# Four row buffers and deeper lookahead in the projection of the second graph's rows

## What is computed

```
x2   = x1 + factor * y[kept position of the row]
xn   = (x2 - mean(x2)) / sqrt(var(x2) + 1e-5)
hh   = xn @ W                       # 8 heads of 32
s_src, s_dst = sum over a head of hh * a_src, hh * a_dst
```

## Time and profile before

| | us |
|---|---|
| runs | 5120.07, 5128.81, 5130.25; median 5128.81 |
| profiled execution | 5127.6 |
| its span, first to last instruction | 5125.8 |
| mean granted TensorE clock | 0.861 of full speed |
| busy: PE, DVE, POOL, ACT | 3909.5, 3118.7, 2344.6, 1867.0 |
| stage `project_heads`, from its first instruction (2562.4) to the next stage's (2733.3) | 170.9 |

### The profile page before, as it was taken

How to read it: one execution, slowest core, us unless ns; L and a number is a source line. 1 busy time by engine, 2 the same in 40 slices (tenths; PEclk the granted TensorE clock), 3 DMA queues, 4 the chain that set the end, 5 groups by cost and what they waited for, 6 DMA issues and landing times. The chain is left out here.

```text
span 5125.8 us, 69922 instructions
## 1 busy us (share of the span) xinstructions
PE 3909.5 (76%) x16154; PEld 2806.8 (55%) x16282; DVE 3118.7 (61%) x7733; ACT 1867.0 (36%) x5097; POOL 2344.6 (46%) x2387
## 2 busy tenths in 40 slices
PE   6977777777777659967965777777774349999998
PEld 3555555555555448856843444444443336777776
DVE  3389989999999766662045777777777761111111
ACT  1334444444444213311213555555553303333332
POOL 2265555556555340001045777777773402333332
PEclk8989999999999789987966778787776569999999
DMA  2565555555555232211064444444443441211111
GB/s 75 182 186 160 164 159 160 161 160 165 162 156 160 66 105 92 92 58 41 31 201 129 110 109 110 108 111 110 111 110 86 132 148 29 33 31 31 31 32 27
DMA packets 316121, 553.59 MB, mean 108 GB/s; under 512 B 63430, under 2 KB 213782, under 8 KB 315856
## 3 DMA queue, kind: packets, MB, share of 16 engines
q0 software_dynamic: 137120, 388.63, 28.9%
q1 hardware_dynamic: 178736, 161.98, 10.4%
HBM read 459.75 MB, written 90.62 MB: 107 GB/s over the span
## 5 line engine op out<-in xcount | busy, mean ns | idle before, releaser
L411 POOL DMA_INDIRECT attend_ring<-kv_rows,all_step_src x880 | 867.5, 986 | 592.5 <-PE attend_ps_agg L450 440.0
L914 POOL DMA_INDIRECT edge_ring<-head_rows,all_step_src x880 | 863.9, 982 | 285.2 <-issue 185.5
L950 PE MATMUL edge_ps_agg<-edge_msg,edge_sel 128*128 128x264 f32 x1760 | 644.7, 492 | 208.3 <-DVE graph_acc L1249 105.7
L450 PE MATMUL attend_ps_agg<-attend_msg,attend_sel 128*128 128x264 f32 x1760 | 591.3, 441 | 243.5 <-DVE graph_qa L766 138.1
L2799 DVE TENSOR_TENSOR moe_gl<-moe_ps_h,moe_act 128x341 f32<-128x341 f32 x210 | 107.9, 514 | 776.7 <-PE moe_ps_h L2717 776.7
L950 PEld LDWEIGHTS edge_ps_agg<-edge_msg,edge_sel 128*128 128x128 f32 x1760 | 374.9, 237 | 352.6 <-issue 171.3
L450 PEld LDWEIGHTS attend_ps_agg<-attend_msg,attend_sel 128*128 128x128 f32 x1760 | 317.7, 204 | 415.3 <-DVE graph_qa L766 182.7
L436 PE MATMUL attend_ps_q<-graph_qa,attend_sel_t 128*128 x1760 | 512.2, 419 | 7.1 <-DVE attend_prod L661 6.4
L2717 PE MATMUL moe_ps_h<-experts_w,moe_xt 128*128 x1680 | 501.8, 451 | 0.6 <-ACT moe_xt L2748 0.6
L766 DVE SCALAR_TENSOR_TENSOR graph_qa<-graph_qa,all_step_same,attend_ps_agg 128x264 f32 x880 | 421.8, 479 | 58.8 <-PE attend_ps_agg L450 42.4
L571 ACT ACTIVATE attend_sel<-all_lane,all_step_dst 128x128 f32<-128x128 f32 x880 | 281.2, 390 | 429.6 <-PE attend_ps_agg L450 414.0
(11 more groups left out here) (423 smaller groups left out, 6374.8 us busy)
## 6 DMA issues: line engine op xcount, KB each, us to landing
attend_ring<-kv_rows,all_step_src POOLq DMA_INDIRECT x880
edge_ring<-head_rows,all_step_src POOLq DMA_INDIRECT x880
kv_rows<-qkv_kv SPq DMA_DIRECT2D x25, 512.0 KB, 2.9
experts_w<-in_w_t SPq DMA_DIRECT2D x16, 682.0 KB
attend_mask<-run_starts SPq DMA_DIRECT2D x440, 8.1 KB
edge_mask<-run_starts SPq DMA_DIRECT2D x440, 8.1 KB
head_rows<-hds_hh SPq DMA_DIRECT2D x25, 264.0 KB, 3.4
qkv_x<-in_x SPq DMA_DIRECT2D x25, 256.0 KB, 3.3
```

The costliest lines, as they stand in the source:

```text
L411: nc.gpsimd.indirect_dma_start(ring[:, step % RING1, :], None, g.kv_rows, bass.IndirectOffsetOnAxis(g.step_src[:, step:step + 1], 0)).then ...
L450: nc.tensor.matmul(ps_agg[i % SUM_BANKS][:, 0:AGG], sel[:, q % 2, u % QU, :], msg[:, q % 2, u % QU, :], start=True, stop=True).then_inc(s_ ...
L914: nc.gpsimd.indirect_dma_start(ring[:, n % slots, u, :], None, g.head_rows, bass.IndirectOffsetOnAxis(g.step_src[:, step:step + 1], 0)).th ...
L950: nc.tensor.matmul(ps_agg[i % BANKS][:, 0:AGG], sel[:, q % 2, u % QU, :], msg[:, q % 2, u % QU, :], start=True, stop=True).then_inc(s_agg, 1)
```

## The change

Only `project_heads` changes. Its tiles `r`, `x2`, `xn` and `stat` get four slots instead of two (pair number modulo 4), the turned rows in SBUF and PSUM three; heads and output PSUM keep two. The row numbers of all 25 pairs are converted by one instruction before the first gather. SP loads pairs 0 to 3 at the start (2 and 3 behind the weights) and pair n+4 when pair n is normalized; it stores the heads of pair n-2 in turn n. POOL gathers pairs 0 to 2 at the start and pair n+3 behind the root of pair n; the gather waits for the sum of the pair that had the slot, no longer for its normalization. DVE folds the vectors first, then begins pair n+1 before it ends pair n; sums and statistics count on a semaphore of their own. PE transposes two pairs ahead of the projection, and ScalarE copies turned rows two ahead. All loops are written out, without the hardware loop. Transfers, sizes, matmuls and arithmetic stay as they are.

```diff
@@ -2045,96 +2045,105 @@
 def project_heads(nc, g, s_dst):
+    ROWS, TURNED = 4, 3
     with Phase(nc, "hds") as m:
         w = m.sb("w", [P, KC, AGG + H])
         vec = m.sb("vec", [P, 2, D])
-        r = m.sb("r", [P, 2, 2, 2, D])
...
+        r = m.sb("r", [P, ROWS, 2, 2, D])
+        x2 = m.sb("x2", [P, ROWS, 2, D])
+        xn = m.sb("xn", [P, ROWS, 2, D])
+        xt = m.sb("xt", [P, TURNED, KC, 2, P])
         hh = m.sb("hh", [P, 2, 2, AGG])
         att = m.sb("att", [P, 2, KC, D])
...
+        stat = m.sb("stat", [P, ROWS, 20])
+        idx = m.sb("idx", [P, BLOCKS], I32)
+        ps_t = [m.ps(f"ps_t{i}", [P, 2, KC, P]) for i in range(TURNED)]
         ps_o = [m.ps(f"ps_o{i}", [P, 2, 512]) for i in range(2)]
...
+        s_w, s_ln, s_sum, s_var, s_rstd, s_t, s_xt, s_mm, s_hh, s_fold, s_idx = (
+            m.sem(k) for k in ("w", "ln", "sum", "var", "rstd", "t", "xt", "mm", "hh", "fold", "idx"))
+        s_y = m.sems_of_pool("y", ROWS)
+        s_x, s_st = ([m.sem(f"{k}{i}") for i in range(ROWS)] for k in ("x", "st"))
+        s_hst = [m.sem(f"hst{i}") for i in range(2)]
         block = m.block()
-        LN = 1 + LN_STEPS
+        BEGIN = LN_STEPS
         @block.sync
         def _(sp):
...
+            def load(n):
+                sp.dma_start(r[:, n % ROWS, 0], pair_rows(g.resid, n)).then_inc(s_x[n % ROWS], 16)
+            def store_heads(n):
+                sp.wait_ge(s_hh, n * 2 + 1)
+                sp.dma_start(pair_rows(g.head_rows, n), hh[:, n % 2]).then_inc(s_hst[n % 2], 16)
+            load(0)
+            load(1)
             sp.dma_start(w[:, :, 0:D], g.W.rearrange("(k p) n -> p k n", p=P)).then_inc(s_w, 16)
             for i, a in enumerate((g.a_src, g.a_dst)):
                 sp.dma_start(vec[:, i, :], spread(a.rearrange("h d -> (h d)"), D)).then_inc(s_w, 16)
...
-                    store_heads(n - 1, 1 - slot)
...
+            load(2)
+            load(3)
+            for n in range(PAIRS):
+                sp.wait_ge(s_ln, n + 1)
+                if n + ROWS < PAIRS:
+                    load(n + ROWS)
+                sp.dma_start(pair_rows(g.norm, n), xn[:, n % ROWS]).then_inc(s_st[n % ROWS], 16)
+                sp.dma_start(pair_rows(g.x2, n), x2[:, n % ROWS]).then_inc(s_st[n % ROWS], 16)
+                if n >= 2:
+                    store_heads(n - 2)
+            store_heads(PAIRS - 2)
+            store_heads(PAIRS - 1)
+            for i in range(ROWS):
+                sp.wait_ge(s_st[i], 32 * -(-(PAIRS - i) // ROWS))
+            for i in range(2):
+                sp.wait_ge(s_hst[i], 16 * -(-(PAIRS - i) // 2))
         @block.gpsimd
         def _(pool):
...
-                pool.wait_ge(s_idx, n + 1)
-                pool.nop(nofuse=True)
+            def gather(n):
+                if n >= ROWS:
+                    pool.wait_ge(s_sum, (n - ROWS) * BEGIN + 1)
                 for b in range(2):
...
+                    nc.gpsimd.indirect_dma_start(r[:, n % ROWS, 1, b, :], None, g.kept_y,
+                                                 bass.IndirectOffsetOnAxis(idx[:, n * 2 + b:n * 2 + b + 1], 0)).then_inc(s_y[n % ROWS], 16)
+            def root(n):
                 pool.wait_ge(s_var, n + 1)
...
+                nc.gpsimd.tensor_tensor(stat[:, n % ROWS, 18:20], stat[:, n % ROWS, 16:18], g.minus_half[:], ALU.pow).then_inc(s_rstd, 1)
+            pool.wait_ge(s_idx, 1)
+            gather(0)
+            gather(1)
+            gather(2)
+            for n in range(PAIRS):
+                root(n)
+                if n + 3 < PAIRS:
+                    gather(n + 3)
         @block.vector
         def _(v):
...
-                    v.wait_ge(s_t, n - 1)
+            def begin(n):
+                c, at = Count(v, s_sum, n, BEGIN), n % ROWS
+                v.wait_ge(s_x[at], (n // ROWS + 1) * 16)
+                v.wait_ge(s_y[at], (n // ROWS + 1) * 32)
+                if n >= ROWS:
+                    v.wait_ge(s_st[at], n // ROWS * 32)
                 for b in range(2):
...
+                    ins = nc.vector.scalar_tensor_tensor(x2[:, at, b, :], r[:, at, 1, b, :], g.factor[:, n * 2 + b:n * 2 + b + 1],
+                                                         r[:, at, 0, b, :], ALU.mult, ALU.add)
                 c.then(ins)
...
+                norm_begin(nc, c, stat[:, at], x2[:, at], s_var)
                 c.done()
+            def end(n):
+                if n >= ROWS:
+                    v.wait_ge(s_t, n - ROWS + 1)
+                v.wait_ge(s_rstd, n + 1)
+                for b in range(2):
+                    ins = nc.vector.tensor_scalar(xn[:, n % ROWS, b, :], x2[:, n % ROWS, b, :], stat[:, n % ROWS, 12 + 2 * b:13 + 2 * b],
+                                                  stat[:, n % ROWS, 18 + b:19 + b], ALU.subtract, ALU.mult)
+                ins.then_inc(s_ln, 1)
             def fold():
@@ -2146,70 +2155,66 @@
                     nc.vector.tensor_reduce(w[:, :, D + i * H:D + (i + 1) * H], att[:, i].rearrange("p k (h d) -> p k h d", h=H),
                                             AX.X, ALU.add).then_inc(s_fold, 1)
-            end(begin(0, 0), 0)
             v.wait_ge(s_w, 48)
             fold()
...
-                    end(begin(n + 1, 1 - slot), 1 - slot)
...
+            begin(0)
+            for n in range(PAIRS):
+                if n + 1 < PAIRS:
+                    begin(n + 1)
+                end(n)
         @block.tensor
         def _(pe):
...
+            def transposes(n):
+                pe.wait_ge(s_ln, n + 1)
+                if n >= TURNED:
+                    pe.wait_ge(s_xt, n - TURNED + 1)
                 for b in range(2):
                     for k in range(KC):
...
+                        last = nc.tensor.transpose(ps_t[n % TURNED][:, b, k, :], xn[:, n % ROWS, b, k * P:(k + 1) * P], g.ident[:])
                 last.then_inc(s_t, 1)
...
+            def project(n):
                 pe.wait_ge(s_xt, n + 1)
...
+                if n >= 2:
                     pe.wait_ge(s_hh, n * 2 - 2)
                 for b in range(2):
                     for k in range(KC):
...
+                        last = nc.tensor.matmul(ps_o[n % 2][:, b, 0:AGG + H], xt[:, n % TURNED, k, b, :], w[:, k, :],
                                                 start=(k == 0), stop=(k == KC - 1))
                 last.then_inc(s_mm, 1)
...
+            pe.wait_ge(s_w, 48)
+            pe.wait_ge(s_fold, 4)
+            transposes(0)
+            transposes(1)
+            for n in range(PAIRS):
+                project(n)
+                if n + 2 < PAIRS:
+                    transposes(n + 2)
         @block.scalar
         def _(act):
...
+            def evac_xt(n):
                 act.wait_ge(s_t, n + 1)
...
-                    act.wait_ge(s_y[slot], (n - slot) * 16)
...
-                    index(n + 2, slot)
+                if n >= TURNED:
+                    act.wait_ge(s_mm, n - TURNED + 1)
+                nc.scalar.activation(xt[:, n % TURNED].rearrange("p k b n -> p b k n"), ps_t[n % TURNED][:], ACT.Copy).then_inc(s_xt, 1)
+            def heads(n):
                 act.wait_ge(s_mm, n + 1)
...
+                if n >= 2:
+                    act.wait_ge(s_hst[n % 2], n // 2 * 16)
+                nc.scalar.activation(hh[:, n % 2], ps_o[n % 2][:, :, 0:AGG], ACT.Copy).then_inc(s_hh, 1)
+                nc.scalar.activation(s_dst[:, n * 2:n * 2 + 2, :], ps_o[n % 2][:, :, AGG:AGG + H], ACT.Copy).then_inc(s_hh, 1)
+            nc.scalar.activation(idx[:], g.from_kept[:], ACT.Copy).then_inc(s_idx, 1)
+            evac_xt(0)
+            evac_xt(1)
+            for n in range(PAIRS):
+                heads(n)
+                if n + 2 < PAIRS:
+                    evac_xt(n + 2)
 def graph2_out(nc, g, acc, logits, out):
```

More of the change, by code:

```diff
@@ L2127, in begin @@
                 for b in range(2):
-                    ins = nc.vector.scalar_tensor_tensor(x2[:, slot, b, :], r[:, slot, 1, b, :],
-                                                         g.factor[:, bass.ds(n * 2 + b, 1)], r[:, slot, 0, b, :],
-                                                         ALU.mult, ALU.add)
+                    ins = nc.vector.scalar_tensor_tensor(x2[:, at, b, :], r[:, at, 1, b, :], g.factor[:, n * 2 + b:n * 2 + b + 1],
+                                                         r[:, at, 0, b, :], ALU.mult, ALU.add)
@@ L2131, in begin @@
                 c.then(ins)
-                norm_begin(nc, c, stat[:, slot], x2[:, slot], s_var)
-                return c
-            def end(c, slot):
-                norm_end(nc, c, stat[:, slot], xn[:, slot], x2[:, slot], s_rstd, 0, 1)
+                norm_begin(nc, c, stat[:, at], x2[:, at], s_var)
                 c.done()
+            def end(n):
[6 more added lines that the diff above has]
+                ins.then_inc(s_ln, 1)
@@ L2177, in turn @@
                     for k in range(KC):
-                        last = nc.tensor.matmul(ps_o[slot][:, b, 0:AGG + H], xt[:, slot, k, b, :], w[:, k, :],
```

(22 more changed lines are left out.)

50 lines of the change are left out of this document (removed).

## The result

Runs of the two kernels in turn gave a median of 5090.8 us for the changed one (5086.7 to 5093.8) and 5126.9 us for the one before (5120.1 to 5130.3). The ratio is 0.9930, with a 95% interval of 0.9915 to 0.9945: 36 us faster. Forecast were 5084 and a range of 5063 to 5105. The profiled execution took 5093.7 us, its span is 5091.8, at a mean granted clock of 0.867.

The account below looks back on a forecast made before the run. A loop of waits bound the stage at 6.30 us a pair; the DMA engines would be next, at p = 4.3 us a pair. Stage gain 44.6, so 5127.6 - 44.6 + 1.2 = 5084 us, range 5063 to 5105.

Parts of the forecast that it names:

- The bound before: Stage before the change: no engine or transfer full, a loop of waits through indices, gathers and landing, 6.30 us a pair.
- Pair time: Changed stage: DMA engines bound, SP's bytes 2.88 plus gathers' packet time 1.36 give 4.24, taken as 4.3 us a pair.
- The loop of three pairs: Changed stage, gathers three ahead: POOL's issue 3.1, landing 3.8 and DVE 2.3 need only 3.1 us a pair, no longer the bound.
- the next bound: POOL in the changed stage: root, gap and two gathers take 3.4 us a pair, 4.1 with DVE working beside it.
- POOL or DVE bounds, p = 3.5: Rival for the changed stage: POOL or DVE sets 3.5 us a pair, gain 65, total 5064; chance 0.22.
- Start: Start of the changed stage: vectors land about 3.5 us behind their issue, first pair normalized at 2576.3.
- ScalarE, SP: Changed stage: heads' store lands 5.1 to 6.6 us after normalization, before the buffer's reuse at 7.1; covered, little to spare.
- The stages behind: Stages after the changed one: same code, so costed at nothing.
- signs of being wrong: Whole kernel: DMA share below 0.85 with p above 5, PE unpausing at 0.50, DVE waiting for stores, later stages changing time.
- depth not reached: Rival for the changed stage: some buffer or SP's order holds about 6 us a pair, gain 5, total 5124; chance 0.05.
- PE stays low: Rival for the changed stage: PE stays at its lower clock, 5.1 us a pair, gain 22, total 5107; chance 0.14.
- transfers pile up: Rival for the changed stage: late stores delay sums, needing 11.7 us landing; at 13 us, 27 us slower, 5156; chance 0.04.

Follow-up runs that it names:

- number 7: Kernel before, loops written out, indices of all pairs converted by one copy and the gathers' wait for them gone; ratio 0.9962, stage 154.9 us.
- 2: Kernel before, with the stage's hardware loops written out as Python loops on all five engines; ratio 1.0009, stage 169.0 us.
- number 5: Kernel before, semaphores declared so that all later ones get the changed kernel's numbers, all work as before; ratio 1.0016, stage 167.2 us.
- number 8: Changed kernel with gathers two pairs ahead instead of three, everything else kept; ratio 0.9957, stage 139.9 us.
- number 3: Changed kernel without the store of x2, the output stage reading the normalized rows instead; ratio 0.992, stage 105.6 us at 3.46 a pair.
- number 6: Changed kernel with 23 idle instructions on POOL behind its last root; ratio 0.9902, stage 110.0 us, edge stage 1417.7 us.
- number 11: Changed kernel again, unaltered, for a second trace; 5441.0 us against 5499.9 for the kernel before, ratio 0.9902.
- number 9: Changed kernel with two pairs gathered at the start instead of three, the third behind the first root; 5499.5 us beside 5493.6 for the kernel before.
- 12: Changed kernel with gathers three pairs ahead up to pair 20 and two ahead for the last four; ratio 0.9896, stage 115.7 us.
- 10: Changed kernel with two more gathers, whose data nobody reads, behind the last root; 5434.0 us beside 5493.6 for the kernel before, stage 112.4 us.

## Why the prediction was right, and where it was not

**The bound before: right.** The stage was a loop of waits. Opening its first edge alone gives 12 to 14 us (number 7 against 2 and 5); taking the normalization out of it as well, with the change's buffers and orders, brings the stage to 139.9 (number 8); the third pair of depth to 110.

**Pair time: the mis-sized term.** The step that failed is "SP's bytes at 367 and the gathers at their packet time give 4.24". Measured are 3.65, almost the lower end of 3.6. What the prediction took for the bound is seen: DMA share over 1, DVE waiting for landings, a shorter pair when bytes go (number 3). But packet time of the gathers isn't engine time of its own beside SP's. Both queues' shares add to 101% over 90 us and to 105% over the 60 fullest, and the total runs at 361 to 371 GB/s with the gathers in it. The microsecond at 229 GB/s, from which I argued, was not full; it was the beginning of a pause. This term is worth (4.3 - 3.65) x 23 = 15.0 us. The Trainium skill (DMA: Bandwidth & Descriptors, Specifications) with its 358 GB/s gave 3.7 us, which in this case was nearer than my sum. The windows pass it, at up to 371 over 20 us; the Trainium skill (HBM Reference, Specifications (TRN2)) calls it the share with both cores of a pair at work, and this program uses one core.

**The loop of three pairs: a wait judged gone that was not.** "So p must be at least (3.1 + 3.8 + 2.3) / 3 = 3.1: no longer the bound" took the landing of a stage whose DMA engines had pauses. With the 5.8 us that the gathers took in the full one, the same formula gives 3.7 (it counts a gather's own 1 us twice, as the view takes landing from the issue). The trace shows this loop closed: from the end of a pair's statistics over root, gathers, landing and the beginning of the pair three later it is 10.99 us in the mean, 3.66 a pair. The root follows its input within 0.2 us in 18 of 24 pairs, and the beginning starts within 0.6 us of the last packet of its gathers in 16 of 22. So the pair's time fits two accounts, full DMA engines and three pairs in flight at the landing that full engines give. Number 3 doesn't part them, as bytes and landing fell together. Gathers four pairs ahead would, and no such kernel ran; the rate of 361 to 371 GB/s, as high as in the full microsecond of the earlier trace rows (367), is why I still put the bytes first.

**POOL: right as the next bound.** I took 3.4 for it; its own work is 0.79 + 2 x 0.995 + 0.49 = 3.27, and number 3 shows it at 3.46 once DMA gives way. The rival "POOL or DVE bounds, p = 3.5" was near in time and wrong in mechanism: DMA and POOL lie 0.2 us apart. The root did not go to the output stage's 957 ns. It went from 728 to 793; 713 when DVE waits beside it and 810 in number 8, where it works. The port rule of the Trainium skill (SBUF — State Buffer, Who interferes with whom) agrees in direction, at 65 to 82 ns here and not at the 230 that I had let it cost.

**PE: the lower clock did not come.** The granted clock was 0.91 and then 1.00 in the windows from 2600 on, and the tail 10.7 us (2667.77 to 2678.45) where I took 13.5 from 11.4 to 18. The projection of a pair took 2.00 us, less than the 2.10 of the earlier trace rows. PE had shorter pauses in each pair than before, and the clock rose; which of the two came first the runs don't separate.

**Start: 1.5 us short.** The vectors landed 5.65 us behind their issue (2570.79 to 2576.44), not 3.5, so the first pair was normalized 15.4 us into the stage instead of 13.9.

**ScalarE, SP: covered, but not as worked out.** At p = 3.65 and a landing of 6.1 the heads' store is late each pair (45.4 us of waiting on ScalarE). The cover was a different one: the 2.7 us until PE needs the output PSUM again.

Together: 44.6 + 15.0 + 2.8 - 1.5 = 60.9, the stage's measured gain.

**The stages behind: the step that failed outright.** "The stages behind are the same code; I cost them at nothing." The edge stage lost 24 us in this profile, 16 to 26 in the three kernels with the change against the three without it at 5122 us. POOL bounds that stage there, and 880 gathers of 27 ns more each in the mean (11 at the median) are 24 us. On the chips where POOL doesn't bound it, the same long gathers cost little (5.7 us in number 6 against 5), and the change gives 59 us (number 11). So the agreement of 5084 with 5090.8 is luck: it comes from errors of opposite sign. Against the profiled execution, in which I expected 5083.0 and which took 5093.7, they are -16.3 in the stage, +24.0 in the edge stage, +6.0 ahead and -3.2 in the rest. Two of the prediction's own signs of being wrong came: the stages behind took another time, and DVE waited for stores, though only 2.5 us.

**What stays open** is why the gathers got longer. All eight kernels with three pairs of gathers ahead, for the whole stage or most of it, have them (957 to 960 ns at the median), all six without have the short ones (946 to 949), number 8 with the same buffers, the same semaphore count, the same order of DVE and PE and as many POOL instructions among them. The semaphore numbers are refuted (number 5), a shift of 23 instructions does not mend it (6), and neither does less depth at the start (9) or the end (12), nor two gathers behind it (10). That is a correlation with no mechanism. How full the stage's DMA engines are doesn't sort them clearly either: number 3, at 297 GB/s, has the long ones, and number 8 the short ones at 1.32 MB in 4.85 us, 272 GB/s. Other depths and other stages with three ahead were not tried.

The rivals "depth not reached", "PE stays low" and "transfers pile up" are refuted by p = 3.65: the buffers reached three pairs, DVE's waits for stores sum to 2.5 us, and the longest landing of a heads' store was 7.2 us, far from 11.7.

## What to carry to other kernels

When a loop of waits is opened, the floor is the total of the bytes over the best saturated rate seen in the trace; packet time of two queues did not add here. Work the loop out with the landing of the loaded stage (5.8 us here), not with that of the idle one (3.8), before you call it gone. Check the stages behind the change by their groups before crediting it with the total, above all where one engine's instruction rate bounds them, and again on another chip. Once transfers bound, one more overlap (here DVE's order, 3 us) buys little, and the next bound may be 5% away.

## What the runs showed of the hardware, unexpected

- The same indirect gather, same form and data, has two durations in the edge stage, depending on the kernel: some 946 or some 957 ns at the median, from the stage's first gather to its last; in the attend stage ahead of the change it is 946 in both kernels.
- Loads, stores and gathers mixed run at 371 GB/s over 20 us, with a DMA share of 1.07.
- Chips differ by 7 to 8% on the same program (5122 against 5494 to 5525 us), in the attend stage (1505 against 1664 us in number 5) and the edge stage (1166 to 1172 against 1408 to 1412 us for forms of the kernel before). The gathers don't explain it: they land as fast there, and the changed stage, which gathers too, takes 110 us on either; the stages behind them take 1221 to 1225 us on each (number 9 apart).
